# Attention with padded keys: the mask moves from the score tiles into K and V

## What is computed

```python
qh = _split_heads(q @ wq.T + bq, h)        # q is x
kh = _split_heads(k @ wk.T + bk, h)        # k and v are the context
vh = _split_heads(v @ wv.T + bv, h)
scores = jnp.einsum('ntd,nsd->nts', qh, kh) / jnp.sqrt(depth)
km = jnp.repeat(mask.astype(scores.dtype), h, axis=0)[:, None, :]
scores = scores + km * PAD                 # PAD = -2**32 + 1
attn = jax.nn.softmax(scores, axis=-1)
ctx = jnp.einsum('nts,nsd->ntd', attn, vh)
out = _merge_heads(ctx, h) + q
mu = jnp.mean(out, axis=-1, keepdims=True)
var = jnp.var(out, axis=-1, keepdims=True)
out = (out - mu) / jnp.sqrt(var + LN_EPS) * gamma + beta
```

## Time and profile before

| what | value |
|---|---|
| median of three runs | 1152.3 us (1148.76 to 1154.68) |
| the profiled execution's own time | 1148.7 us |
| its span, first to last instruction | 1146.9 us |
| busy: TensorE matmul, weight load | 1117.5 us (97%), 1033.1 us (90%) |
| busy: VectorE, ScalarE, GpSimd | 908.4 us (79%), 614.2 us (54%), 858.7 us (75%) |
| mean granted TensorE clock | 0.994 of full speed |

### The profile page before, as it was taken

How to read it: one execution, slowest core, us unless ns; L and a number is a source line. 1 busy time by engine, 2 the same in 40 slices (tenths; PEclk the granted TensorE clock), 3 DMA queues, 4 the chain that set the end, 5 groups by cost and what they waited for, 6 DMA issues and landing times.

```text
span 1146.9 us, 25924 instructions
## 1 busy us (share of the span) xinstructions
PE 1117.5 (97%) x7536; PEld 1033.1 (90%) x7536; DVE 908.4 (79%) x1677; ACT 614.2 (54%) x1003; POOL 858.7 (75%) x709
## 2 busy tenths in 40 slices
PE   7999899999999999999999999999999999999994
PEld 7888699999999999999999999999999999999983
DVE  5233678888888888888888888888888888888787
ACT  5221355555565665555555565665555555565551
POOL 1310335888888888888888888888888888888886
PEclk9999999999999999999999999999999999999997
DMA  7756233324333344433334333344433334333223
GB/s 258 271 189 243 68 91 91 123 76 126 115 103 114 117 126 126 126 117 124 91 107 125 116 98 118 115 126 126 126 117 115 103 104 125 111 104 118 81 83 137
DMA packets 146885, 141.98 MB, mean 124 GB/s; under 512 B 86404, under 2 KB 87428, under 8 KB 146852
## 3 DMA queue, kind: packets, MB, share of 16 engines
q1 hardware_dynamic: 146852, 141.56, 39.2%
HBM read 92.65 MB, written 48.85 MB: 123 GB/s over the span
## 4 chain that ended last, share of the span: by engine, by line
PE 84%; DVE 3%; POOL 1%; issue 0%; ACT 0%; DVEq 0%; POOLq 0%
PE q_ps L613 31%; PE o_ps L654 23%; PE s_ps L629 18%; PE t_ps L640 12%; POOL probs L899 1%; DVE row_max L796 0%; DVE stats L719 0%; DVE probs L788 0%; DVE attn L750 0%; DVE y L759 0%; DVE q_lo L778 0%; PE q_ps L654 0%; POOL y L879 0%; POOL y L876 0%; DVE y L765 0%
## 5 line engine op out<-in xcount | busy, mean ns | idle before, releaser
L899 POOL TENSOR_TENSOR probs<-probs,row_max 128x616 f32<-128x616 f32 x255 | 310.5, 1218 | 157.3 <-DVE row_max L796 157.3
L931 ACT ACTIVATE probs<-probs 128x616 f32<-128x616 f32 x256 | 183.3, 716 | 270.1 <-POOL probs L899 267.7
L654 PE MATMUL o_ps<-v_tiles,pt 128*128 128x66 f32 x2520 | 310.4, 270 | 2.7 <-DVE attn L711 2.7
L654 PEld LDWEIGHTS o_ps<-v_tiles,pt 128*128 128x128 f32 x2520 | 303.8, 192 | 3.1 <-issue 3.1
L629 PE MATMUL s_ps<-bd,q_hi 128*128 128x308 f32 x1024 | 260.5, 305 | 0.6 <-issue 0.6
L788 DVE TENSOR_TENSOR probs<-s_ps,mask_pad 128x616 f32<-128x616 f32 x256 | 203.3, 794 | 52.7 <-PE s_ps L629 51.3
L613 PE MATMUL q_ps<-x_lo,wq_hi 128*128 128x512 f32 x500 | 217.8, 436 | 3.3 <-PEq L135 2.1
L796 DVE TENSOR_REDUCE row_max<-probs 128x8 f32<-128x616 f32 x256 | 202.4, 790 | 12.1
L613 PE MATMUL q_ps<-x_hi,wq_lo 128*128 128x512 f32 x500 | 197.3, 395 | 0.0
L613 PE MATMUL q_ps<-x_hi,wq_hi 128*128 128x512 f32 x500 | 197.1, 394 | 0.0
L629 PEld LDWEIGHTS s_ps<-bd,q_hi 128*128 128x128 f32 x1024 | 180.7, 188 | 12.4 <-issue 1.0
(11 more groups left out here) (82 smaller groups left out, 1299.7 us busy)
## 6 DMA issues: line engine op xcount, KB each, us to landing
xT_raw<-in_xT SPq DMA_DIRECT2D x128, 256.0 KB, 3.4
x_rows<-in_x SPq DMA_DIRECT2D x32, 1024.0 KB, 5.7
out<-y SPq DMA_DIRECT2D x128, 256.0 KB, 2.1
k_scratch<-k_out SPq DMA_DIRECT2D x8, 1232.0 KB, 5.5
bd<-k_scratch SPq DMA_DIRECT2D x128, 77.0 KB, 2.4
v_scratch<-v_out SPq DMA_DIRECT2D x16, 264.0 KB
v_tiles<-v_scratch SPq DMA_DIRECT2D x256, 9.9 KB
ctx_raw<-in_ctxT SPq DMA_DIRECT2D x3, 1232.0 KB, 8.2
```

The costliest lines, as they stand in the source:

```text
L654: mm = pe.matmul(bank_of(b, t)[:, col:col + tile_cols[i]], pt[h][0:w, i, P * t:P * t + P], v_tiles[v_buffer(b, h)][0:w, i, 0:tile_cols[i]] ...
L899: pool.tensor_tensor(v, v, row_max[:, u, :].unsqueeze(2).broadcast_to([P, HH, S]), ALU.subtract).then_inc(shifted, 1)
L931: act.activation(probs[h][:, t, :], probs[h][:, t, :], ACT.Exp).then_inc(exp_done, 1)
```

## The change

The mask leaves phase two. In phase one a pattern keep (1 for a key that counts, 0 for padding) multiplies K with its bias as it leaves PSUM (VectorE, centre_of_keys); VectorE sums the kept keys of each head and feature (k_sum), GpSimd subtracts their mean from the kept ones (k_shift, then k_part; the shift changes no softmax), so that a masked key has a score of 0 and the others are centred around it. ScalarE copies the high part from k_part in SBUF, VectorE takes the low part from there. V is multiplied by the keep pattern on GpSimd after its bias, and the ones beside V become the keep pattern, so masked keys drop out of product and sum. In a mask row without any kept key all V rows are kept.

The keep pattern comes by five transfers that ScalarE issues first of all. VectorE counts keys and prepares the rows; TensorE turns them (turn_keep, five small transposes in v_ps[3]) after the second group of keys of half 1; ScalarE copies the result (keep_v) ahead of all keys, and its high(c + 1) and the high part of wv now stand ahead of the keys too. The low parts of half 0 stand between the centred groups of half 1 on VectorE, those of half 1 between the V tiles. K's banks are free at k_masked, V's at v_biased. SP's load of the context of c + 2 stands behind the second K store of chunk c, and the load of the second x moved from chunk 2 to chunk 3.

In phase two VectorE takes the maximum straight from PSUM and subtracts it while reading PSUM, which gives the bank free; GpSimd has the splits of x instead of the subtraction.

```diff
@@ SP, phase one
-                for i in range(2):
-                    sp.dma_start(mask_pad[i][:].bitcast(I32), mask[i].partition_broadcast(P)).then_inc(mask_loaded, DMA)
                 for c in range(CHUNKS):
                     store_keys(c, 0)
-                    if 1 < c + 1 < CHUNKS:
-                        load(c + 1)
                     store_keys(c, 1)
+                    if c + 2 < CHUNKS:
+                        load(c + 2)
...
-                    if c == 2:
+                    if c == 3:
                         sp.wait_ge(x_hi_ready, KC)
                         sp.wait_ge(x_lo_ready, KC)
...
@@ GpSimd, phase one
+                def centre_keys(c, half):
+                    for m in range(NG):
+                        n = (2 * c + half) * NG + m
+                        pool.wait_ge(k_summed, n + 1)
+                        at_least(pool, k_ready, n)
+                        pool.tensor_tensor(k_shift[:], shift_of_key[:, m, :, :].unsqueeze(1).broadcast_to([P, HB // 2, 2, S]),
+                                           k_sum[:, n % KS, :, :].unsqueeze(3).broadcast_to([P, HB // 2, 2, S]),
+                                           ALU.mult).then_inc(k_shift_ready, 1)
+                        pool.wait_ge(k_shift_ready, n + 1)
+                        pool.tensor_tensor(k_part[:, n % KS, :, :, :], k_part[:, n % KS, :, :, :], k_shift[:], ALU.add
+                                           ).then_inc(k_ready, 1)
...
+                for c in range(CHUNKS):
+                    centre_keys(c, 0)
+                    centre_keys(c, 1)
+                    keep_values(c)
...
@@ ScalarE, phase one
+                for q in range(HG):
+                    act.dma_start(keep[DH * q:DH * q + DH, :, :, :].bitcast(I32).rearrange("p g i s -> p g (i s)"),
+                                 mask_heads[q].partition_broadcast(DH)).then_inc(mask_loaded, DMA)
+                act.dma_start(keep_h[:].bitcast(I32), mask).then_inc(mask_loaded, DMA)
...
+                act.wait_ge(wv_loaded, DMA)
+                act.copy(wv_hi[:], w_raw[:]).then_inc(wv_hi_ready, 1)
+                act.wait_ge(keep_turned, 1)
+                for j in range(VT):
+                    act.copy(keep_v[0:v_n[j], j, :], v_ps[3][0:v_n[j], HEADS * j:HEADS * j + HEADS]
+                             ).then_inc(keep_v_ready, 1)
...
@@ VectorE, phase one
+                def centre_of_keys(n):
+                    c, half, m = n // (2 * NG), n // NG % 2, n % NG
+                    slot = n % KS
+                    dve.wait_ge(k_done, n + 1)
+                    at_least(dve, k_copied, n + 1 - KS)
+                    dve.scalar_tensor_tensor(out=k_part[:, slot, :, :, :].rearrange("p c i s -> p c (i s)"),
+                                             in0=k_ps[m][:, 0:HR].rearrange("p (c r) -> p c r", r=2 * S),
+                                             scalar=bk_sc[:, m:m + 1], in1=keep_of(m),
+                                             op0=ALU.add, op1=ALU.mult).then_inc(k_masked, 1)
+                    dve.wait_ge(k_masked, n + 1)
+                    dve.tensor_reduce(k_sum[:, slot, :, :], k_part[:, slot, :, :, :], AX.X, ALU.add
+                                      ).then_inc(k_summed, 1)
...
+                def keys(c, half):
+                    first = 2 * c * NG
+                    for n in range(first + half * NG, first + half * NG + NG):
+                        centre_of_keys(n)
+                        if half == 1:
+                            low_keys_out(n - NG)
...
-                                          ALU.add).then_inc(v_copied, 1)
+                                          ALU.add).then_inc(v_biased, 1)
+                        if j < NG:
+                            low_keys_out(2 * c * NG + NG + j)
...
@@ TensorE
+                def turn_keep():
+                    pe.wait_ge(ident_set, 1)
+                    pe.wait_ge(rows_step, 3)
+                    for j in range(VT):
+                        mm = pe.transpose(v_ps[3][0:v_n[j], HEADS * j:HEADS * j + HEADS],
+                                          keep_rows[:].rearrange("h c i s -> h (c i s)")[:, P * j:P * j + v_n[j]],
+                                          ident[0:HEADS, 0:HEADS])
+                    mm.then_inc(keep_turned, 1)
...
-                            pe.wait_ge(k_copied, (2 * c + half - 1) * NG + m + 1)
+                            pe.wait_ge(k_masked, (2 * c + half - 1) * NG + m + 1)
...
+                            if (c, half, m) == (0, 1, 1):
+                                turn_keep()
...
-                    at_least(pe, masked, b * 8 + (4 * h + t - 1))
+                    at_least(pe, shifted, b * 8 + (4 * h + t - 1))
@@ VectorE, phase two
-                        if real(a):
-                            add_mask(a, h, t, par)
-                        if 4 <= s <= 6 and real(a + 2):
-                            split_x(a + 2, s - 3, par)
...
                         if real(a):
                             maximum(a, h, t)
-                        if is_last(a) and s == 7:
-                            subtract_last_max()
                         if rows is not None:
                             mean_and_var(*rows)
+                        if real(a):
+                            subtract_max(a, h, t)
@@ GpSimd, phase two
+                        if 3 <= s <= 6 and real(a + 2):
+                            split_x(a + 2, s - 3, par)
```

187 lines of the change are left out of this document (107 added, 80 removed).

## The result

The changed kernel took 1159.0 us (median of 4 runs, 1158.65 to 1159.35); the kernel before, run beside it, 1152.1 us (4 runs, 1148.76 to 1154.68). The ratio is 1.0062, with a 95% interval of 1.0041 to 1.0082: slower by 7 us or 0.6%, where 1157.1 us (+4.8) was forecast and 1150 to 1164 was the range. The profiled run took 1158.8 us, its span is 1156.9.

A forecast was written before the change was run, and what follows sets the result against it. TensorE was taken to bound the kernel, busy for all 943.00 us of the steady stretch, leaving start, phase passage and tail. Terms 2.8 + 0.3 + 2.8 + 0.9 - 2.0 = +4.8 us on 1152.3 gave 1157.1 us, range 1150 to 1164.

The forecast's parts named there:

- Steady part 0: Phase two, steady part: lighter VectorE and GpSimd gain nothing beside busy TensorE; 0 taken, bounds 0 to +3 us.
- Start +2.8: Kernel start: mask transfers, the wait for the keep rows and their transposes, less a removed wait, add 2.8 us.
- The wait of the old code at 14.36: Start: TensorE's wait for the first low part of K goes, as the mask multiplication comes no later; -0.25 us.
- The wait for the keep rows: Start: TensorE waits for VectorE's rows_step before turn_keep, 1.7 us (1.0 to 2.5).
- Within phase one +0.3: Phase one after the start: added VectorE and GpSimd work is mostly covered; +0.3 us, bounds 0 to +1.5.
- Both fit: Phase one, per key group: VectorE's 1.42 us and GpSimd's 1.2 to 1.6 us fit within TensorE's 1.70 us.
- Rival 2: First two chunks of phase one: VectorE falls behind, TensorE loses 3 to 8 us more, 1160 to 1165; chance 0.17.
- The contention that the prediction cited: Phase one: low parts with two SBUF inputs could each wait a whole GpSimd operation, sum 2 to 3 us higher.
- End of phase one +2.8: End of phase one: the last K store, four xT loads and five V stores drain in 11.5 us; +2.8 us.
- First steps +0.9: First steps of phase two: GpSimd's splits delay xT loads, partly offset by shorter q_lo waits; +0.9 us (0 to +2.5).
- Tail -2.0: Tail: one VectorE step fewer and a shorter wait for GpSimd's sum of rows save 2.0 us, range -1 to -3.
- The sum +4.8: Whole kernel: the terms for start, phase one, its end, first steps and tail add up to +4.8 us.

The follow-up runs named there:

- run 3: Changed kernel with the five mask transfers issued by SP behind the first context loads instead of by ScalarE: 1159.0 us, ratio 1.0047 to the kernel before.
- run 11: Kernel before with idle matmuls alone, eight at the end of phase one and twelve in the tail: 1150.9 us, ratio 0.9992.
- run 5: Changed kernel with nine idle matmuls ahead of the transposes of the keep rows: 1158.4 us, ratio 1.0046 to the kernel before.
- run 1: Changed kernel with turn_keep behind the fourth group of keys of the second half instead of the second: 1159.0 us, ratio 1.0057 to the kernel before.
- run 7: Changed kernel with turn_keep two key groups later and ScalarE's high(1) ahead of the keep_v copies: 1160.1 us, ratio 1.0066 to the kernel before.
- run 9: Changed kernel as in run 7, with bd0 zeroes ahead of the masks, x_lo0 on VectorE, context loads ahead of K stores: 1156.8 us, ratio 1.0048.
- Run 2: Changed kernel with the load of the second x back in the third chunk, one chunk earlier: 1156.1 us, ratio 1.0025 to the kernel before.
- Run 8: Changed kernel with the low parts of x in phase two back on VectorE: 1158.7 us, ratio 1.0056 to the kernel before.
- run 12: Changed kernel with twenty idle matmuls of 512 columns at the end of phase one: 1162.2 us, ratio 1.0078 to the kernel before.
- Run 6: Changed kernel with twelve idle matmuls ahead of the last block's product with V of the third query tile: 1157.25 us, ratio 1.0041.
- run 4: The kernel before once more, unchanged, for its spread and a second profile: 1152.1 us, ratio 0.9992.

## Why the prediction was right, and where it was not

**Steady part 0: right.** 943.00 us of 943.00, with 0.80 us for either operation on PSUM.

**Start +2.8: too low; it was 5.1.** Its parts: the mask transfers 0.96 (0.8 said). ScalarE was through with them and the table load at 4.41 us, as the prediction had it; what came last was the context data, slower to land beside them, which it had named without a price (run 3). The wait of the old code at 14.36 is gone (-0.25, right). The wait for the keep rows 1.49 (1.7 said), the transposes 0.37 (0.5 said). Not in the sum at all is the clock: at the low level for 19 of the first matmuls where it was for 12, 0.84 us, and low again behind the wait, where 24 matmuls took 5.03 us instead of 3.4: 1.6 us. Together 2.4 us. The first of the two is no price of the change: the three profiles of the kernel before, with the same start, have 12, 16 and 22 matmuls at the low level (22 in run 11), and those of the changed kernel and its variants 14 to 22. The prediction weighed the clock at one place only, the end of phase one. It should have done so behind every wait that it added. Yet by run 5 the 1.6 us behind the wait were time that other engines needed as well: without them, 0.36 us are won.

**Within phase one +0.3: it was 0.57, and its reasoning was wrong.** The prediction took 0.61 to 0.78 us for each of GpSimd's two operations per key group. In this chunk they took 0.70 and 0.97, after a first pair of 1.28 and 0.85, and the cadence of the chain in the trace is 1.89 us per key group, more than TensorE's 1.70:

```profile
L282 POOL TENSOR_TENSOR k_part<-k_part,k_shift 128x308 f32<-128x308 f32 x5 | 4.7, 946 | 0.4
L278 POOL TENSOR_TENSOR k_shift<-shift_of_key,k_sum 128x308 f32<-128x308 f32 x5 | 4.1, 817 | 0.6
```

"Both fit" was therefore false in a stretch with keys alone, and only the V tiles, in which GpSimd can catch up, kept it out of TensorE's waits. Run 1 and run 7 made it visible. The lateness of 5.1 us at the start is what hid it: the changed kernel waits 0.3 us in phase one only because TensorE arrives late. Rival 2 had this place, with VectorE as the engine; by runs 1, 7 and 9 it is the chain of GpSimd, ScalarE and VectorE, with SP's order of loads in the second chunk, and its price is a loss of gains, not 3 to 8 us more.

The contention that the prediction cited has rows now, here in run 7, GpSimd's timeline and VectorE's:

```profile
59.71 0.85 POOL L282 TENSOR_TENSOR k_part<-k_part,k_shift 128x308 f32<-128x308 f32 x1
```

```profile
59.95 0.95 DVE L399 TENSOR_TENSOR k_out<-k_part,k_out 128x308 fp32r<-128x308 f32 x1
```

VectorE's subtraction of two SBUF operands takes 0.47 us with GpSimd idle (58.61 in the same run). Started at 59.95 in the middle of GpSimd's addition, which ends at 60.56, it takes 0.95: it stands still for what is left of the addition, 0.5 us. GpSimd's addition takes 0.85 us, and 0.97 where it starts ahead of the end of such a subtraction. The largest case is `shift_of_key`: it starts during VectorE's keep_rows and then has wv_lo (2.27 us) in front of it; 3.90 us for 616 columns, of which some 1.1 remain once wv_lo is done. The Trainium skill (SBUF — State Buffer, Who interferes with whom) has the two engines share a pair of ports under an exclusive lock, with the issue order deciding who is blocked. The trace agrees for the pair of lines above. At `shift_of_key` start times alone would not tell it: GpSimd's instruction starts at 20.19 us in the changed kernel, wv_lo at 20.73, and it is GpSimd that waits. What the prediction made of it was the price: a low part loses 0.2 to 0.5 us, the rest of a GpSimd operation and not a whole one, and the case that hurt, GpSimd blocked by VectorE at the start of its chain, was in no term.

**End of phase one +2.8: right in kind, 3.78 measured.** One K store, four xT loads and five V stores took from 122.2 to 133.4 us, 11.2 us where 11.5 were taken from the earlier trace rows. What was off is when it began: the store left 5.9 us after the old-time 116.3, of which 5.67 is the lag; and between the end of the DMA traffic and TensorE's first matmul lay 1.6 us. The 0.6 that the prediction took for this step was measured behind VectorE's last work, not behind a transfer. Run 2 took the loads out and gave back 2.9 us, as its expectation had it.

**First steps +0.9: 0.74 measured, by the path named.** The wait on the first scores was 1.28 us, where 2 to 3 was said. GpSimd's splits ended at about 143.4 us, and SP's loads for the third x left at 143.50 against 131.48 before: 12.0 us later, in a stage that itself began 9.45 later, so 2.6 us, within the 2.0 to 2.7 said; part of that went into shorter waits for q_lo, as said. Run 8 took this cause away and gained 1.7 to 2.0 us there. The clock at the low level from 131 to 138 us cost the first steps 1.38 us and was hidden by the wait behind them, as said; yet runs 2 and 12 show that the statement is only half of it, since the wait that grows when the first steps are quick can bring the clock down in its turn.

**Tail -2.0: -0.2 measured, and the clock is why.** The gain was there: at the first y of the last batch's end the lag had shrunk from 10.2 to 7.75 us (VectorE at 1117.72 before, 1125.47 after), 2.45 us. Then TensorE, sooner done with its part, waited 2.50 us for VectorE's attn, where it had waited 0.35, the clock fell, and transposes and products that now stood on the path ran at the low level (0.66 in 1130 to 1135). Run 6 filled the wait and had 1.6 us of it back, and run 1's profile, with the wait but without the fall, had as much. What failed was to treat VectorE's work in the tail as a row of its own: TensorE is a link in it, at the speed of the clock. How much the tail won depends on the two profiles that are compared, since both kernels have a fall there: 0.2 us against the first profile of the kernel before, 1.8 if the changed kernel's clock stays up, and 2.9 against run 4's profile.

**The base.** The sum +4.8 was made against the quickest execution of the kernel before (1148.7 us, clock 0.994), and run 4 shows what the others have in addition: the clock's falls after 2.09 us at the end of phase one and a longer one after 1.29 us in the tail. In the first profile the clock did not fall at the first place, and at the second it was low for some 3 us only. The changed kernel has such falls in its profiled run too, so that part is not added twice: +10.0 us against the quick profile, +5.4 against run 4's, +6.9 between the medians. Against the profile on which it was built the sum is therefore too low by 5.2 us, and its errors all but add up: 2.3 at the start, 0.3 within phase one, 1.0 at its end and 1.8 in the tail, against 0.2 the other way in the first steps. Some 4 us of the 5.2 are the clock (2.4 at the start, 1.6 in the tail), 1.0 is the step behind the last transfer. That 4.8 came near the 6.9 of the medians is luck in so far as the median of the kernel before holds falls of the clock that its first profile lacked. Near run 4's +5.4, where both kernels are at a mean clock of 0.989, it came with a tail that won more and a stretch up to the first product with V that lost more than said, 8.2 us instead of 6.8.

## What to carry to other kernels

Price each wait that a change adds or lengthens twice: its length, and the matmuls behind it at half the clock; and do the same for a wait that grows because something before it got faster. When a step is moved off one engine, ask for that engine's queue at the new place (memsets, a K store ahead of a load) before its length, and if a removed wait comes back elsewhere with the same length, look for the chain that paces both. Idle matmuls in a pause are a cheap probe: they tell a clock's cost from the wait's own. They have to stand in the wait behind which the clock falls, which need not be the same in two kernels (run 11), and they can move a fall to the next wait (run 12). And compare two kernels at the same mean granted clock before a difference of a few us is put down to the code.

## What the runs showed of the hardware

The granted clock did not follow from a pause's length alone. It fell behind waits of 1.30 us (in the tails of all three profiles of the kernel before), 1.49 us (at 20.95), 1.83 us (run 7) and 5.87 us. Behind pauses of 2.09 us, of 2.4 to 2.6 us and of 2.50 us in the tail it fell in one profile and stayed in another (rows before against run 4, run 12 against run 2, the changed kernel against run 1). At the start, too, the number of matmuls at the low level differed between executions with the same start: 12, 16 and 22. The same kernel, on the same chip, had executions from 1148.5 to 1154.7 us, in the order of their mean granted clock (run 4), and with idle matmuls in two places the spread was 1.0 us.

The Trainium skill (TensorE: Matmul & The Clock Gate, Why this matters for your kernels) warns of idle gaps between bursts of matmuls. The traces agree that the clock falls behind gaps, and show that it did so in one execution and not in the next. That made up most of the 5.2 us by which the sum missed the profiled difference.
